# Keys and values of a gated cross-attention block by seven block products instead of eight

## The reference

```
T = 8 * 256 tokens, D = 1024
K = context @ wk      # [2048, 1024], 8 heads of 128, then rotated (RoPE)
V = context @ wv      # [2048, 1024], 8 heads of 128
q = rope(LN(x) @ wq)  # 32 heads; heads 4g..4g+3 share key head g
y = softmax(q K^T * scale + mask) V @ wo
```

## Time and profile before

| | |
|---|---|
| time, median of 3 runs | 2992.04 us (2989.24 to 2992.15) |
| profiled execution, span from first to last instruction | 2990.3 us |
| PE busy in the span | 2959.3 us (99%), 14701 matmuls |
| DVE, ACT, POOL busy | 2009.8, 1282.8, 1369.9 us |
| granted TensorE clock, mean | 0.998 of full |
| DMA, mean | 163 GB/s |

### The profile page before, as it was taken

How to read it: one execution, slowest core, us unless ns; L and a number is a source line. 1 busy time by engine, 2 the same in 40 slices (tenths; PEclk the granted TensorE clock), 3 DMA queues, 4 the chain that set the end, 5 groups by cost and what they waited for, 6 DMA issues and landing times.

```text
span 2990.3 us, 41114 instructions
## 1 busy us (share of the span) xinstructions
PE 2959.3 (99%) x14701; PEld 2482.3 (83%) x14701; DVE 2009.8 (67%) x4714; ACT 1282.8 (43%) x2686; POOL 1369.9 (46%) x1105
## 2 busy tenths in 40 slices
PE   9999999999999999999999999999999999999999
PEld 7888878887788878887888888888888888888887
DVE  4432478888655686679667777666776676666566
ACT  4111366665422422232223666555555545544332
POOL 2422388886422587777776334322322211111264
PEclk9999999999999999999999999999999999999999
DMA  7332421212555564455444787676677666665531
GB/s 254 127 120 99 166 70 50 78 64 75 191 177 166 197 179 113 113 149 152 109 112 120 242 268 239 227 242 209 193 221 244 189 196 204 208 194 166 225 108 76
DMA packets 320661, 488.29 MB, mean 163 GB/s; under 512 B 26236, under 2 KB 155644, under 8 KB 317644
## 3 DMA queue, kind: packets, MB, share of 16 engines
q1 hardware_dynamic: 319740, 484.23, 51.0%
q10 hardware_dynamic: 720, 1.44, 0.1%
HBM read 324.12 MB, written 161.48 MB: 162 GB/s over the span
## 4 chain that ended last, share of the span: by engine, by line
PE 61%; DVE 3%; DMA 0%; issue 0%; POOL 0%; ACT 0%; SPq 0%; DVEq 0%; ACTq 0%
PE PB L150 19%; PE PB L151 19%; PE PB L152 19%; PE PB L2401 4%; DVE qp_b L2150 1%; PE PB L2830 0%; DVE PB L2192 0%; DMA qp_raw<-in_wq 0%; DVE qp_r L2198 0%; DVE PB L2174 0%; DVE qp_c L2194 0%; DVE qp_r L2188 0%; DVE qp_r L2189 0%; POOL f1x L3046 0%; DMA qp_in<-xod 0%
## 5 line engine op out<-in xcount | busy, mean ns | idle before, releaser
L2567 POOL TENSOR_TENSOR at_ql<-at_qf,at_qh 128x512 fp32r<-128x512 f32 x128 | 166.2, 1299 | 833.9 <-ACT at_qh L2441 833.9
L2448 ACT ACTIVATE at_ss<-at_ss,at_sm,at_bs 128x256 f32<-128x256 f32 x512 | 301.9, 591 | 317.1 <-DVE at_sm L2528 317.1
L150 PE MATMUL PB<-at_woh,at_ah 128*128 128x512 f32 x1024 | 400.4, 391 | 0.6 <-DVE at_al L2550 0.6
L151 PE MATMUL PB<-at_wol,at_ah 128*128 128x512 f32 x1024 | 399.9, 390 | 0.0
L152 PE MATMUL PB<-at_woh,at_al 128*128 128x512 f32 x1024 | 399.5, 390 | 0.0
L2558 DVE SCALAR_TENSOR_TENSOR at_xt<-PB,gt,at_xt 128x512 f32<-128x512 f32 x256 | 192.1, 750 | 249.7 <-PE PB L152 249.5
L150 PE MATMUL PB<-qp_b,qp_a 128*128 128x512 f32 x896 | 350.2, 391 | 8.4 <-DVE qp_r L2196 3.8
L151 PE MATMUL PB<-qp_b,qp_a 128*128 128x512 f32 x896 | 349.3, 390 | 0.0
L152 PE MATMUL PB<-qp_b,qp_a 128*128 128x512 f32 x896 | 349.2, 390 | 0.0
L2220 POOL TENSOR_TENSOR qp_a<-qp_raw,qp_a 128x512 fp32r<-128x512 f32 x192 | 260.0, 1364 | 101.2 <-ACT qp_a L2112 98.5
L2112 ACT ACTIVATE qp_a<-qp_raw 128x512 fp32r<-128x512 f32 x192 | 113.5, 625 | 292.1 <-POOL qp_raw L2224 162.4
(11 more groups left out here) (314 smaller groups left out, 7570.6 us busy)
## 6 DMA issues: line engine op xcount, KB each, us to landing
at_woh<-wod SPq DMA_DIRECT2D x48, 1024.0 KB, 7.4
at_wol<-wod SPq DMA_DIRECT2D x48, 1024.0 KB, 9.6
qp_raw<-in_wq SPq DMA_DIRECT2D x32, 1024.0 KB, 5.4
qd<-qp_r SPq DMA_DIRECT2D x256, 128.0 KB, 2.5
at_qf<-qd SPq DMA_DIRECT2D x128, 256.0 KB, 3.4
at_rawo<-in_wo SPq DMA_DIRECT2D x32, 512.0 KB, 5.3
wod<-at_woh SPq DMA_DIRECT2D x16, 1024.0 KB, 5.5
wod<-at_wol SPq DMA_DIRECT2D x16, 1024.0 KB, 6.3
```

What stands on the lines that cost most here:

```text
L150: pe.matmul(o, ah, bh, start=start, stop=False)
L151: pe.matmul(o, ah, bl, start=False, stop=False)
L2448: m = act.activation(at_ss[s][:, c, :], at_ss[s][:, c, :], ACT.Exp, bias=z[:, 4 + c:5 + c], scale=at_bs[:, qn % 2, 8 + 2 * b + c % 2:9 + 2 ...
L2567: self.pool.tensor_tensor(at_ql[n % 3][:, :], at_qf[n % 2][:, :], asf(at_qh[n % 3][:, :]), ALU.subtract).then_inc(*inc("at_pool", ("q", n)))
```

## The change

K and V are computed as blocks. The context is cut into 1024 tokens x 512 of the inner dimension and so on: with A (tokens, by halves of 512 of a block of 1024 tokens, times halves of the inner dimension) and B (the weight, 2 x 2 blocks of 512 x 512), the four blocks of the product come from seven block products (Strassen's scheme in Winograd's form) in place of eight. Per weight there are two such passes (1024 tokens each), four passes in all, and 7 x 4 = 28 products n = 0 to 27. A product has four output tiles t = 0 to 3 (128 x 512) and four chunks c of the inner dimension, so 4 x 4 x 3 = 48 matmuls.

- The operands are no longer resident: each product splits its two factors anew into a ring of 10 chunks, ACT the high part, **DVE every low part** (both sides), six chunks ahead of the product (`prepare`).
- The token sums S1 to S4 run on GpSimd, in passes 0 and 2 (16 instructions each), the weight sums T1 to T4 on DVE (16 in each pass). They go with `prepare` of products k = 1 to 4 of a pass.
- Where they can, products go on in the bank of an earlier one (`kv_goes_on`), so that the bank holds the sum. Results leave a bank by an ACT copy (k = 0, 2, 3, 6) or a DVE addition (k = 1, 4, 5).
- The first three products (n < 3) run chunk by chunk over all four tiles, the others tile by tile.
- K and V are stored once, in fp32, and K not rotated. In attention, GpSimd rotates the keys of a group (`turn_k`, three instructions, from K and a copy of K with the halves swapped by the load), and K and V are split there: high by ACT, low by GpSimd.
- The handover to ac is regrouped: ac's second and third piece now stand behind product 25, the fourth and fifth behind half of product 26, the sixth behind half of product 27.

The core of the diff (removed kv functions, the placement of buffers and the renamed waits of ac are left out):

```diff
-        kd = [nc.dram_tensor(f"kd{i}", [G, P, T], F, kind="Internal").ap() for i in range(2)]
+        kd = nc.dram_tensor("kd", [G, P, T], F, kind="Internal").ap()
+        KV_SEQ = (0, 4, 3, 1, 6, 2, 5)
+        KV_PASSES = (("v", 0), ("k", 0), ("k", 1), ("v", 1))
+        KV_N = 7 * len(KV_PASSES)
+        KV_RING = 10
+        KV_FACTOR = {"a": ("a11", "s2", "a21", "s1", "a12", "a22", "s4"), "b": ("b11", "b11", "b12", "t1", "b21", "b21", "b22")}
+        KV_SUM = {("a", 3): "S1", ("a", 1): "S2", ("a", 2): "S3", ("a", 6): "S4", ("b", 3): "T1", ("b", 1): "T2", ("b", 2): "T3", ("b", 5): "T4"}
+        def kv_bank(n, t):
+            if n >= KV_N - 2:
+                return 4 + t % 2
+            return 4 * ((n // 7 + (n % 7 in (1, 2, 4))) % 2) + t
+        def kv_goes_on(n):
+            return n % 7 in (3, 4) or n % 7 in (5, 6) and n < KV_N - 2
+        def kv_emptied(n, t):
+            return ("kv_act" if n % 7 in (0, 2, 3) or n % 7 == 6 and n < KV_N - 2 else "kv_dve", ("out", n, t))
+        def kv_schedule(do):
+            do.begin()
+            for q in range(6):
+                do.prepare(q // 4, q % 4)
+            for n in range(KV_N):
+                do.product(n)
+                for t in range(4):
+                    if 4 * n + 6 + t < 4 * KV_N:
+                        do.prepare(n + 1 + (2 + t) // 4, (2 + t) % 4)
+                    do.tile(n, t)
+                    do.leave(n, t)
+                    do.load(n, t)
+                    if n >= KV_N - 2 and t % 2 and (n, t) != (KV_N - 1, 3):
+                        yield
+                if KV_N - 5 < n < KV_N - 2:
+                    yield
+        class KvTensor(Keys):
+            def product(self, n):
+                if n < 3:
+                    for c in range(1 if n == 0 else 0, 4):
+                        for t in range(4):
+                            if c == 0:
+                                self.claim(n, t)
+                            self.chunk(n, t, c)
+            def tile(self, n, t):
+                if n > 2:
+                    self.claim(n, t)
+                    for c in range(4):
+                        self.chunk(n, t, c)
...
+        class KvVector(Keys):
+            def weight_sums(self, p, k, c):
...
+                if k == 1:
+                    on.wait_ge(*at(*kv_loaded("b11", p, c)))
+                    on.wait_ge(*at(*kv_loaded("b12", p, c)))
...
+                    dve.tensor_tensor(t1, b12, b11, ALU.subtract).then_inc(*inc("kv_dve", ("T1", p, c)))
+                if k == 2:
+                    on.wait_ge(*at(*kv_loaded("b22", p, c)))
...
+                    dve.tensor_tensor(b11, b22, t1, ALU.subtract).then_inc(*inc("kv_dve", ("T2", p, c)))
+                if k == 3:
...
+                    dve.tensor_tensor(b12, b22, b12, ALU.subtract).then_inc(*inc("kv_dve", ("T3", p, c)))
...
+            def prepare(self, n, c):
+                on, p, k = self.on, n // 7, n % 7
+                for side in ("a", "b"):
+                    on.wait_ge(*at("kv_act", (side, n, c)))
+                    self.dve.tensor_tensor(kv_part(side, n, c, 1), kv_factor(side, n, c), asf(kv_part(side, n, c, 0)), ALU.subtract).then_inc(
+                        *inc("kv_dve", (side, n, c)))
+                self.weight_sums(p, k, c)
+            def leave(self, n, t):
...
+                if k == 1:
+                    on.wait_ge(*at("kv_pe", ("out", n, t)))
+                    on.wait_ge(*at("kv_act", ("out", n - 1, t)))
+                    dve.tensor_tensor(c11, c11, bank, ALU.add).then_inc(*inc("kv_dve", ("out", n, t)))
...
+        class KvGpsimd(Keys):
+            def token_sums(self, p, k, c):
...
+                    pool.tensor_tensor(s1, a21, a22, ALU.add).then_inc(*inc("kv_pool", ("S1", p, c)))
...
+                    pool.tensor_tensor(s2, s1, a11, ALU.subtract).then_inc(*inc("kv_pool", ("S2", p, c)))
...
+                    pool.tensor_tensor(s4, a12, s2, ALU.subtract).then_inc(*inc("kv_pool", ("S4", p, c)))
...
+                    pool.tensor_tensor(a21, a11, a21, ALU.subtract).then_inc(*inc("kv_pool", ("S3", p, c)))
+        class KvSync(Keys):
+            def begin(self):
+                for c in range(4):
+                    self.fetch("b11", 0, c)
+                for c in range(4):
+                    self.fetch("a12", 0, c)
+                    self.fetch("b21", 0, c)
+                for c in range(4):
+                    self.fetch("b12", 0, c)
+                    self.fetch("a21", 0, c)
+                    self.fetch("a22", 0, c)
+                for c in range(4):
+                    self.fetch("b22", 0, c)
...
 at_schedule
+            do.turn_k(0)
             yield
             for n in range(2):
                 do.split_q(n)
                 do.fetch_q(n + 2)
+            do.split_k(0)
+            do.split_v(0)
...
+                n = u // 4 + 1
+                if u % 4 == 3 and n < NG:
+                    do.split_k(n)
                 if u + 2 < NU:
                     do.split_q(u + 2)
...
                 do.split_wo(u)
+                if u % 4 == 2 and n < NG:
+                    do.turn_k(n)
+                if u % 4 == 0 and 0 < u < NU:
+                    do.split_v(u // 4)
...
 AtTensor.scores
-                    on.wait_ge(*at(f"at_k{n % 2}", ("low", n)))
+                    on.wait_ge(*at("at_act", ("k", n)))
+                    on.wait_ge(*at("at_pool", ("k", n)))
...
 AtGpsimd
+            def turn_k(self, n):
...
+                on.wait_ge(*at(f"at_k{n % 2}", ("swapped", n, 1)))
+                pool.tensor_tensor(kr[:, :, :], kr[:, :, :], cosine, ALU.mult).then_inc(*inc("at_pool", ("cosine", n)))
+                pool.tensor_tensor(ks[:, :, :], ks[:, :, :], sine, ALU.mult).then_inc(*inc("at_pool", ("sine", n)))
+                on.wait_ge(*at("at_pool", ("sine", n)))
+                pool.tensor_tensor(kr[:, :, :], kr[:, :, :], ks[:, :, :], ALU.subtract).then_inc(*inc("at_pool", ("turned", n)))
+            def split_k(self, n):
+                self.on.wait_ge(*at("at_act", ("k", n)))
+                self.pool.tensor_tensor(at_kl[n % 2][:, :], at_kr[n % 2][:, :, :].rearrange("p b n -> p (b n)"), asf(at_kh[n % 2][:, :]),
+                                        ALU.subtract).then_inc(*inc("at_pool", ("k", n)))
...
 weave
             next(kv)
             next(ac)
-            for beside in (2, 2, 1):
-                next(kv)
-                next(kv)
-                for _ in range(beside):
-                    next(ac)
+            next(kv)
+            next(ac)
+            next(ac)
+            next(kv)
+            next(ac)
+            next(ac)
+            next(kv)
+            next(kv)
+            next(ac)
```

More of the change, by code:

```diff
@@ L211, in flamingo @@
[L211 to L226, removed]
@@ new lines, in flamingo, with none, __init__, claim @@
+        class Keys:
+            def none(self, *args):
+                pass
+            begin = prepare = product = tile = leave = load = none
+        class KvTensor(Keys):
+            def __init__(self, pe, on, spare):
+                self.pe, self.on, self.spare = pe, on, spare
+            def claim(self, n, t):
+                for e in self.spare[kv_bank(n, t)]:
+                    self.on.wait_ge(*at(*e))
+                self.spare[kv_bank(n, t)] = [kv_emptied(n, t)]
+            def begin(self):
+                pe, on = self.pe, self.on
+                on.wait_ge(*at("kv_pool", "zeros"))
+                for _ in range(3):
+                    pe.matmul(BK[0], kv_f[0][:, 0:P], kv_f[0][:, :], start=True, stop=True)
+                for j in range(3):
+                    for t in range(4):
+                        if j == 0:
+                            on.wait_ge(*at("kv_act", ("a", 0, 0)))
+                            on.wait_ge(*at("kv_act", ("b", 0, 0)))
+                            self.claim(0, t)
+                        else:
+                            on.wait_ge(*at("kv_dve", ("ab"[j - 1], 0, 0)))
+                        m = pe.matmul(BK[kv_bank(0, t)], kv_part("a", 0, 0, j % 2)[:, P * t:P * t + P], kv_part("b", 0, 0, j // 2), start=j == 0, stop=False)
+                m.then_inc(*inc("kv_pe", ("chunk", 0, 0)))
+            def chunk(self, n, t, c):
+                on, ts = self.on, slice(P * t, P * t + P)
+                for side in ("a", "b"):
+                    on.wait_ge(*at("kv_act", (side, n, c)))
+                    on.wait_ge(*at("kv_dve", (side, n, c)))
+                rows, cols = ("a", "b") if KV_PASSES[n // 7][0] == "v" else ("b", "a")
+                m = three(self.pe, BK[kv_bank(n, t)], (kv_part(rows, n, c, 0)[:, ts], kv_part(rows, n, c, 1)[:, ts]),
+                          (kv_part(cols, n, c, 0), kv_part(cols, n, c, 1)), c == 0 and not kv_goes_on(n), c == 3, kv_goes_on(n))
+                if c == 3:
+                    m.then_inc(*inc("kv_pe", ("out", n, t)))
+                elif t == 3:
+                    m.then_inc(*inc("kv_pe", ("chunk", n, c)))
```

(11 more changed lines are left out.)

542 lines of the change are left out of this document (224 added, 318 removed).

## The result

| | before | after |
|---|---|---|
| time, median of 5 runs | 2992.04 us | 3001.92 us (2998.39 to 3003.13) |
| ratio of the times | | 1.0032, 95% interval 1.0021 to 1.0044 |
| profiled execution, span | 2990.3 us | 3000.3 us |

What follows compares the result with a forecast made beforehand. TensorE's matmul count was taken to bound the kernel, all else in kv hidden. 2990.3 - 43.5 + 19 + 2 + 2.1 + 1.3 + 1 = 2972.2, with the median 1.7 above: 2974 us, range 2959 to 2988.

Steps and rivals of the forecast that it cites:

- Term 1: K and V matmuls: 1344 in place of 1536, each 0.2266 us, so -43.5 us.
- Term 2: Third product: TensorE waits for DVE's PSUM additions, delayed where DVE instructions meet GpSimd's token sums; +19 us (5 to 28).
- that case: Third product: all 16 GpSimd sums meet a DVE split, DVE's last addition ends at 53.5, a stall of 22.7 us.
- The 334 GB/s behind the first sum: Start of kv: load rate taken for `b12`, by which DVE's first weight sum starts at 16 us.
- The clock behind it: After the third product's stall: one drop from 2.4 to 1.2 GHz, +2 us (0 to 4).
- The rest of kv: Later products of K and V: splits, sums and exits hidden beside the matmuls; 0 us (0 to 3).
- Term 3: Handover to ac: work behind product 25's end E takes 10.2 us, TensorE has 8.16 beside it; +2.1 us (0 to 4).
- Term 4: Entry to attention: the key's low part stands behind `at_ql`, so the scores start late by +1.3 us (0 to 3).
- Term 5: Attention, steady state: GpSimd's turning and splits end in time and are hidden, except in first groups; +1 us (0 to 4).
- rival A: Attention: GpSimd low parts, each lasting d = 2.25 us, stall each of 31 groups by 2d - 3.47; 32 us, 3006; chance 0.07.
- "Stores and loads of K and V are halved": Attention: less traffic for K and V, worth 0 since no wait of TensorE names it.

Runs made afterwards that it cites:

- e8: e7 with DVE's statistics of x moved behind product 24 and GpSimd's part ahead of its context split; 2964.0 us, ratio 0.9910 to the kernel before.
- e4: Changed kernel with the keys in attention rotated for one column only, so GpSimd's turning has next to no length; 2982.4 us, ratio 0.9972 to the kernel before.
- e3: Changed kernel, but GpSimd waits for DVE's softmax weights ahead of the key's low part (`at_kl`); 2988.0 us, ratio 0.9989 to the kernel before.
- e7: Changed kernel with product 1's DVE additions first, `b12` loaded earlier, sums S2 and S4 delayed, GpSimd's key low part behind DVE's weights; 2971.3 us, ratio 0.9941.
- e9: Changed kernel, but GpSimd waits for DVE's weights only ahead of `at_wol`, in each group's last unit; 2987.7 us, ratio 0.9987 to the kernel before.
- e1: Changed kernel with GpSimd's token sums computed for one column in 512, so next to no length; 2983.6 us, ratio 0.9969 to the kernel before.

## Why the prediction was wrong

**Wrong in sign and range: 2974 (2959 to 2988) was forecast, 3001.9 measured.** By its terms:

- Term 1, -43.5: right. 192 matmuls fewer, and product 7 to 21 took 154.0 us for 672 matmuls, 1.4 of it the wait on `kv_b` in product 15.
- Term 2, +19: right in place and mechanism; that the waits sum to 18.1 us is partly luck. The 19 took off four of the 16 meetings, which puts the last exit at 49.7 us. All 16 took place, and it ended at 52.5, near the 53.5 of that case. TensorE did its tiles between the waits, half as fast, so that not all of this delay shows as waits. (The 334 GB/s behind the first sum stands in no row; the 329 of the earlier trace rows gives 16.2 us in place of 16.0, and it started at 16.50.)
- The clock behind it, +2 (0 to 4): the mechanism right, the size not. 23.5 - 18.1 leaves 5.4 us, and 8.58 us of work at 0.50 make 4.3 of them, since the clock stayed low through all four waits, not for one stretch of 5 us like the earlier trace rows. The other 1.1 is a start 0.16 us later, 0.3 us of delays in product 1, and what lies between the drawn end of a matmul and the start of the next.
- The rest of kv, 0 (0 to 3): 1.7.
- Term 3, +2.1 (0 to 4): 6.8. `ac_ql` ended at 326.6, E + 11.5 rather than 10.2, since one of DVE's splits took 2.88 us beside GpSimd's `ac_cl`. The wait was 3.3 and a second one 0.8; the low clock behind the first, which this term didn't have, takes most of the rest.
- Term 4, +1.3: 1.3.
- **Term 5, +1 (0 to 4): 18.3. This is the step that failed.** It said "Slack 1.4 and 0.9 us, so hidden". The low parts were indeed in time; TensorE waited for the queries' by 0.5 us in all, at two places. But I asked only when GpSimd's new instructions end, and not whom they hold up while they run. Term 2 had that very question for kv, with the earlier trace rows beside it, and I didn't put it to attention, where DVE's weights stand on TensorE's path. The rival A had the place and the sign (GpSimd's work in attention), but as slow low parts in all 31 groups; it came in three units, through DVE, and while DVE still had the last products of the queries. (Later one more unit took 3.38 us, beside the turning itself, and cost a wait of 0.9.) (Rival A's sum puts the end of the gain at d = 2.1; 2d - 3.47 = 18 / 31 gives 2.03.)
- "Stores and loads of K and V are halved": the stores are, the loads aren't. Per group three blocks are loaded in place of four, since K is loaded twice, once with its halves swapped. No wait of TensorE names them, so the 0 stands.

The low clock alone, behind waits, took 4.3 us at the start and 6.8 in attention, where I had charged 2 in all. Had Term 5 stood at 18.3 and nothing else been changed, the forecast would have been 2991; with what the start lost behind its waits (5.4) and with the handover (6.8) too, 2999.

Left open: 1.9 us between f0 and the first scores (TensorE waited 4.3 us in place of 3.0 on `f0xn`, and the granted clock was 0.66 from 780 to 790 us where the kernel before had 0.83 from 793 to 803; no run tested it), and why from first scores to last output e8 takes 1206.1 us and e4 1201.0, with only 2.5 us of waits more to show for it (1.5 on `at_ql`, 0.7 on ACT's `at_pth`, 0.3 on a load). Part of it is the turning, which e4 leaves out: at 1945 us the weights of a unit took 3.25 us in e8, and the 0.7 us at 1949 us stand behind it.

## What to carry to other kernels

When work goes to an engine that has time to spare, ask of each new instruction not only when it must end but which instruction of the neighbour it holds up, and whether that one stands on the critical path: GpSimd's 4 us per group were in time and still cost 18 us, through DVE. Put such work behind the neighbour's deadline with a wait (e3; in e7 the gain was small), or shorten the row of instructions there (e9). And charge each new idle time of TensorE of some us with the lower clock behind it, here some 4 us on 18.1 of waits and 6.8 on 8.7.

## What the runs showed of the hardware that I had not expected

- DVE and GpSimd took turns instruction by instruction. `tensor_scalar` inside SBUF, 0.34 us alone, took 1.44, 1.36 and 2.43 us beside GpSimd instructions of 1.30, 1.32 and 2.39, which were not lengthened. `tensor_tensor` with two SBUF operands took 1.75 and lengthened GpSimd's from 1.30 to 1.69. With one operand in PSUM it took 0.67 beside a busy GpSimd.
- A start 0.01 us behind GpSimd's gave 5.33 us, one 1.1 us ahead of it 1.14 (changed kernel and e4).
- The granted clock stayed at 0.50 for over 20 us while TensorE did twelve matmuls between waits, and for 6.8 us in e1 (33.8 to 40.6), where the four waits were 0.4 to 1.4 us.
